# A decoder layer's attention projection in rounded products, its MLP weights in sixteen pieces, and identity products at the start

## The chip, the cores and the metric

The kernel runs on one core of one Trainium2 chip. The metric is the device time of one execution in microseconds; the time before is 995.11 us, the median of 3 runs (992.35 to 997.25).

## The reference, cut to what matters

Three blocks, each added to the stream x of shape (4, 512, 256). The first is a gated linear recurrence, the second an attention-free mixing block with an MLP, the third the two-layer local-attention block, which the change is about:

```python
def _layer(x, wqkv, qs, ksc, wo, lg, lb, w1, b1, w2, b2):   # twice, on layernorm(x)
    h = shift_token(x); q, k, v = split(h @ wqkv, 3)         # 8 heads of 64
    q, k = rotary_xpos(l2norm(q) * qs, l2norm(k) * ksc)
    o = local_attention(q, k, v)                             # windows of 128, one window back
    x = x + o @ wo                                           # wo: 512 x 256
    h = layernorm(shift_token(x)) * lg + lb
    a, g = split(h @ w1 + b1, 2)                             # 2 x 682 columns
    return x + (a * gelu(g)) @ w2 + b2
```

All arrays are fp32. In the kernel most products are made from operands split in two, a rounded part (hi, type fp32r) and the rest (lo): hi·hi + hi·lo + lo·hi, three rounded products in place of one full fp32 product.

## The kernel before, in words

All is written by hand: one instruction list for each engine, with semaphores; the order in each list is the order of execution. The activations stay in SBUF; 16 token tiles of 128 rows (4 sequences of 4 tiles) are the windows n of the attention. For each layer l the windows run first, n = 16 l to 16 l + 15, and then four MLP blocks m of 512 tokens. w = n mod 4 is the place in the sequence; at w = 0 a window has half the keys, so half the scores.

TensorE's `window` (L1943) holds, in order: the scores of n, the weighting of values of n-1, two of three qkv products of n+2, the transposes of keys of n+1, of probabilities, of queries of n+1, of the spread reciprocals of the row sums (`transpose_sums`), the third qkv product, the transpose of x for n+3, and last the projection `project_o` of n-1 (L1932 to L1941): four full fp32 products of 128 x 128 by 128 x 256. After the last window come `weigh_values` and `project_o` once more, the waits for the MLP's weights, and the MLP loop.

VectorE's `window` (L1071) masks the scores, writes o_t of n-1 (`normalise`, L1063), norms the keys of n+1 (L1039), inverts the row sums, makes the rotary products of n+2, and adds the projection to the residual (L1069). GpSimd's `window` (L601) copies an x tile (L543), spreads the inverted sums (L558), adds the rotary halves (L551), computes the inverse norms (L569, a power) and the queries' norm (L573), and at w = 1 to 3 splits a third of a quarter of the MLP's weights (L576 to L585): 12 pieces of 356 columns a layer. After the windows it zeroes a row, and `last_columns` (L592) copies the last 42 columns of w1. ScalarE makes the exponentials and most copies out of PSUM.

SyncE issues all DMAs from one list (L364 to L385): the four quarters of the MLP's weights, each into `w_stage` after the quarter before is split; the shifts of the residual by one token (`shift`, L342, lines L351 and L352); `stack_weights` (L319), which puts parts of w2's last rows into one tile; the next layer's qkv and output weights (`load_att`, L306); and after each MLP block's first step `stack_last` (L335), which TensorE waits for before L2017. At the start TensorE waits for the identity (L1664), transposes the first normalised batch, and multiplies it with W_in (`inputs`, L1605); GpSimd splits the gate weights (L437, L439) with the second batch's rstd (L411) between the first and second pair.

Of the kernel before, what the change touches and what calls it, by code (L numbers as in the profile page):

```python
# [41 lines left out]
WM_PIECES = 3  # L42
WM_PIECE = 356
# [32 lines left out]
def build(nc, x, ctx_in, cols_in, rows_in, w_in, w_gate, w_out, wq, wk, wv, wo_x, pos_bias,  # L76
          w1_x, w2_x, lcols_in, qk_scale, rope, wqkv, wo_l, wm_l, out):
    with ExitStack() as ctx:
# [3 lines left out]
        def signals(names):  # L82
# [21 lines left out]
        w_stage = sb("w_stage", [P, KD * 3 * INNER])  # L104
# [3 lines left out]
        wo_sb = sb("wo_sb", [P, KI, D])  # L108
# [100 lines left out]
        o_t = sb("o_t", [P, KI, P], stack=st_att)  # L209
# [3 lines left out]
        probs_t_far = w_stage[:, 2 * KD * INNER:4 * KD * INNER // 2 + 2 * 4 * P].rearrange(  # L213
            "p (i c t) -> p i c t", i=2, t=P)
        probs_ts = [(probs_t, probs_t_far)[i // 2][:, i % 2, :, :] for i in range(KI)]
        st_att.close()
# [32 lines left out]
        (rope_in, wqkv_in, wo_in, wm_in, wq_hi, wq_lo, wm_copied, wm_split, c_xt_lo, d_full, d_in_hi, d_in_lo,  # L249
         d_hi) = signals(  # L250
            "rope_in wqkv_in wo_in wm_in wq_hi wq_lo wm_copied wm_split c_xt_lo d_full d_in_hi d_in_lo d_hi")
# [25 lines left out]
        def _(sp):  # L277
# [28 lines left out]
            def load_att(l):  # L306
                if l:
                    sp.wait_ge(c_pv, l * NT)
                sp.dma_start(w_stage[:, :], wqkv[l].rearrange("p k n -> p (k n)")).then_inc(wqkv_in, 16)
                if l:  # L310
                    sp.wait_ge(c_wo, l * NT)
                sp.dma_start(wo_sb[:, :, :], wo_l[l]).then_inc(wo_in, 16)

            def load_mlp(l, b):

                sp.dma_start(w_stage[:, 0:WM_QUARTER], wm_l[l, :, b * WM_QUARTER:(b + 1) * WM_QUARTER])\
                    .then_inc(wm_in, 16)

            def stack_weights(l):  # L319

                hi, lo = (w[:, W1_COLS + (KH - 1) * D:W1_COLS + KH * D].bitcast(F32) for w in (wm_hi, wm_lo))
                dst = w2_last[:, :].bitcast(F32)
                sp.wait_ge(wm_split, WM_PIECES * NB * (l + 1))
# [64 lines left out]
        def _(pool):  # L388
# [187 lines left out]
            def split_mlp_weights(l, b, piece):  # L576

                m = l * NB + b
                src = w_stage[:, piece * WM_PIECE:(piece + 1) * WM_PIECE]
                dst = bass.ds(b * WM_QUARTER + piece * WM_PIECE, WM_PIECE)  # L580
                wait_alone(pool, wm_in, 16 * m + 16)
                pool.tensor_copy(wm_hi[:, dst], src).then_inc(wm_copied, 1)
                pool.wait_ge(wm_copied, WM_PIECES * m + piece + 1)
                pool.tensor_tensor(wm_lo[:, dst], src, wm_hi[:, dst].bitcast(F32), ALU.subtract)\
                    .then_inc(wm_split, 1)  # L585
# [6 lines left out]
            def last_columns(l):  # L592

                pool.wait_ge(wm_split, WM_PIECES * NB * (l + 1))
# [5 lines left out]

            def window(n, t, w, l, b, two, three):  # L601
                if three:
                    copy_tile(n + 3, t + 3, (w + 3) % 2, l * NB + b + 1 if w == 0 else l * NB + b + 2)
                spread_sums(n)
# [6 lines left out]
                if w:  # L611
                    split_mlp_weights(l, b, w - 1)
# [33 lines left out]
            for l in range(LAYERS):  # L646
# [941 lines left out]
        def _(pe):  # L1588
# [75 lines left out]
            pe.wait_ge(ready_consts, 1)  # L1664
            transpose_in(0)
# [266 lines left out]
            def project_o(n, keyed):  # L1932

                pe.wait_ge(c_ot_out, n + 1)
# [4 lines left out]
                for k in range(KI):  # L1939
                    ins = pe.matmul(bank[2][:, 0:D], o_t[:, k, :], wo_sb[:, k, :], start=(k == 0), stop=(k == KI - 1))  # L1940
                ins.then_inc(c_wo, 1)  # L1941

            def window(n, w, l, prev, one, two, three):  # L1943
# [22 lines left out]
                if prev:  # L1966
                    project_o(n - 1, one)
# [99 lines left out]
            for l in range(LAYERS):  # L2067
                n0 = l * NT
                ahead(l, 7)
                pe.wait_ge(wo_in, 16 * l + 16)  # L2070
# [11 lines left out]
                project_o(n0 + NT - 1, False)  # L2082
                pe.wait_ge(wm_split, WM_PIECES * NB * (l + 1))
# [87 lines left out]
```

## Time and profile before

| | |
|---|---|
| median of 3 runs | 995.11 us (992.35 to 997.25) |
| profiled execution: its time, its span | 999.37 us, 997.6 us |
| mean granted TensorE clock | 0.979 |
| VectorE, ScalarE, GpSimd busy | 674.6, 513.4, 419.3 us |
| attention of layer 0 and layer 1 | about 367 to 578 us and 689 to 895 us |

The page's slices, 40 equal parts of the span, each digit a busy share in tenths; PEclk is the granted clock of TensorE in tenths of full speed:

```
POOL 5333354113121367666666400007676767631110
PEclk9889998999999988999999999999999999989999
```

GpSimd is at 6 to 7 tenths in the attention of both layers and nearly idle in the MLPs. Times in rows are microseconds from the span's start; a duration of a TensorE row runs to the modelled end of the pipeline, so consecutive products overlap, and the distance of their starts is what one costs.

### The profile page before, as it was taken

The numbers are of one execution on the slowest core, as the hardware profiler recorded it, in microseconds if no ns is written. First come the engines' busy times: TensorE is split into PE (matmuls) and PEld (weight loads), VectorE is DVE, ScalarE is ACT, GpSimd is POOL, SyncE is SP. The second block draws the span as 40 slices with busy tenths as digits, with TensorE's granted clock in tenths as the row PEclk, the third lists the DMA queues.
The fourth block names the chain that finished last, engine by engine and source line by source line (L and its number), as shares of the span: only waits on it lengthen the run. The fifth ranks groups of instructions, "written<-read, shape, count | busy, mean of one in ns | idle before, by whom it ended". The sixth has DMA issues, their size and how long they took to land.

```text
span 997.6 us, 17519 instructions
## 1 busy us (share of the span) xinstructions
PE 927.7 (93%) x5688; PEld 776.2 (78%) x5688; DVE 674.6 (68%) x1706; ACT 513.4 (51%) x1221; POOL 419.3 (42%) x420
## 2 busy tenths in 40 slices
PE   5889996999999988999999799999999999889998
PEld 4668875787878867888888678887888888778887
DVE  6778697568687677666777555567776767735553
ACT  5466751313131416767676634454766666654443
POOL 5333354113121367666666400007676767631110
PEclk9889998999999999999999999999999999989999
DMA  7100123000000000000001030000000000000001
GB/s 267 62 1 27 37 64 111 0 2 0 0 1 1 2 21 1 2 22 0 22 0 33 13 103 14 4 26 1 2 24 0 22 0 20 20 14 16 31 24 46
DMA packets 15716, 26.34 MB, mean 26 GB/s; under 512 B 1642, under 2 KB 12256, under 8 KB 14896
## 3 DMA queue, kind: packets, MB, share of 16 engines
q1 hardware_dynamic: 15664, 25.69, 7.9%
q8 instruction: 27, 0.44, 0.2%
q14 instruction: 25, 0.20, 0.1%
HBM read 20.53 MB, written 2.10 MB: 23 GB/s over the span
## 4 chain that ended last, share of the span: by engine, by line
PE 70%; DVE 10%; ACT 8%; issue 4%; POOL 3%; SPq 3%; DMA 2%; ACTq 0%; DVEq 0%; POOLq 0%
PE bank L1592 32%; PE bank L1940 6%; PE bank L1894 5%; PE bank L1800 5%; PE bank L1918 5%; ACT probs L1460 3%; PE bank L1904 3%; PE bank L1881 2%; PE bank L1763 2%; PE bank L1746 1%; PE bank L1928 1%; SPq L352 1%; DVE y L820 1%; PE bank L2013 1%; PE bank L2010 1%
## 5 line engine op out<-in xcount | busy, mean ns | idle before, releaser
L1460 ACT ACTIVATE probs<-bank,row_min 128x256 f32<-128x256 f32 (+1 forms) x256 | 110.4, 458 | 122.2 <-DVE row_min L1048 122.2
L569 POOL TENSOR_TENSOR norms<-norms,minus_half 128x16 f32<-128x16 f32 x32 | 93.6, 2924 | 2.7
L1048 DVE CUSTOM_DVE_ANT_0 bank<-bank,mask 128x256 f32<-128x256 f32 (+1 forms) x256 | 90.7, 425 | 5.7 <-PE bank L1894 5.6
L1592 PE MATMUL bank<-wqkv_hi,x_hi 128*128 128x512 f32 x192 | 82.3, 429 | 1.8 <-DVE rot L1024 1.1
L1592 PE MATMUL bank<-wqkv_lo,x_hi 128*128 128x512 f32 x192 | 76.4, 398 | 0.0
L1592 PE MATMUL bank<-wqkv_hi,x_lo 128*128 128x512 f32 x192 | 75.6, 394 | 0.0
L1185 DVE SCALAR_TENSOR_TENSOR hidden<-bank,lcols,hidden 128x512 f32<-128x512 f32 (+1 forms) x48 | 36.0, 749 | 51.0 <-PE bank L1592 28.3
L1069 DVE TENSOR_TENSOR inner<-inner,bank 128x256 f32 (+1 forms) x32 | 13.5, 421 | 82.0 <-PE bank L1940 82.0
L1904 PE MATMUL bank<-ident,probs 128*128 128x128 f32 x448 | 62.0, 280 | 3.9 <-ACT probs L1460 3.9
L551 POOL TENSOR_TENSOR q_tok<-rot 128x512 f32<-128x512 f32 x32 | 41.2, 1287 | 57.6 <-DVE rot L1024 57.6
L1592 PE MATMUL bank<-t_lo,wm_hi 128*128 128x512 f32 x160 | 63.6, 397 | 0.0
L1592 PE MATMUL bank<-t_hi,wm_hi 128*128 128x512 f32 x160 | 63.6, 397 | 0.0
L1940 PE MATMUL bank<-wo_sb,o_t 128*128 128x256 f32 x256 | 61.5, 383 | 2.0 <-DVE o_t L1063 1.7
L1592 PE MATMUL bank<-t_hi,wm_lo 128*128 128x512 f32 x160 | 62.7, 392 | 0.0
L1894 PE MATMUL bank<-k_t,q_t 64*128 64x256 f32 (+1 forms) x512 | 57.9, 366 | 0.7 <-ACT q_t L1447 0.7
L1800 PE MATMUL bank<-w,ff 128*128 128x256 f32 x256 | 56.7, 379 | 0.0
L1904 PEld LDWEIGHTS bank<-ident,probs 128*128 128x128 f32 x448 | 52.5, 144 | 4.9 <-ACT probs L1460 4.9
L558 POOL COPY rsum_heads<-row_rsum 128x512 f32<-128x512 f32 x32 | 19.6, 614 | 86.4 <-DVE row_rsum L1055 58.5
L1460 ACT ACTIVATION_READ_ACCUMULATOR probs<-bank,row_min 128x1 f32 x256 | 55.5, 217 | 0.0
L1894 PEld LDWEIGHTS bank<-k_t,q_t 64*128 64x128 f32 x512 | 43.4, 189 | 13.9 <-issue 10.7
L1800 PEld LDWEIGHTS bank<-w,ff 128*128 128x128 f32 x256 | 48.5, 190 | 6.6
L1019 DVE TENSOR_TENSOR rot<-bank,rope_l 128x512 f32<-128x512 f32 x64 | 43.8, 685 | 13.7 <-ACT squares L1431 13.7
(253 smaller groups left out, 2663.6 us busy)
## 6 DMA issues: line engine op xcount, KB each, us to landing
w_stage<-in_wm_l_dram SPq DMA_DIRECT2D x8, 534.0 KB, 3.5
w_stage<-in_wqkv_dram SPq DMA_DIRECT2D x2, 1536.0 KB, 8.2
out_dram<-stream SPq DMA_DIRECT2D x8, 256.0 KB, 2.4
emb<-in_ctx_dram SPq DMA_DIRECT2D x1, 1536.0 KB, 6.7
inner<-in_w_gate_dram SPq DMA_DIRECT2D x1, 1152.0 KB, 10.0
stream<-in_x_dram SPq DMA_DIRECT2D x2, 512.0 KB, 5.6
stream<-in_x_dram SPq DMA_DIRECT2D x1, 1024.0 KB, 12.4
ew<-in_pos_bias_dram SPq DMA_DIRECT2D x1, 1024.0 KB, 11.3
```

Of the source, the lines that this page charges most:

```text
L551: pool.tensor_tensor(dst[:, par, :], rot[:, 2 * i, :], rot[:, 2 * i + 1, :], ALU.add)\
L569: pool.tensor_tensor(norms[:, 2, :], norms[:, 1, :], minus_half[:, :], ALU.pow).then_inc(c_rn, 1)
L1019: dve.tensor_tensor(rot[:, 2 * i, :].rearrange("p (h d) -> p h d", d=DH), src, cos, ALU.mult)\
L1048: dve.tensor_tensor_reduce(logits, logits, mask[:, 2 * P - nk:2 * P], 1.0, FAR, ALU.add, ALU.min, row_min[:, w % 2, 2 * i + e:2 * i + e + ...
L1185: dve.scalar_tensor_tensor(hidden[0:r, i % 2, :], up[0:r, :], lcols[0:r, l, L_B1A + j:L_B1A + j + 1], hidden[0:r, i % 2, :], ALU.add, ALU. ...
L1460: act.activation(probs[:, i, e, 0:nk], logits, ACT.Exp, bias=row_min[:, w % 2, h:h + 1], scale=-1.0, accum_out=row_sum[:, w % 2, h:h + 1]) ...
L1592: ins = pe.matmul(out, stationary, moving, start=(first and i == 0), stop=(last and i == len(terms) - 1))
L1800: ins = pe.matmul(bank[6 + t // 2][:, (t % 2) * D:(t % 2 + 1) * D], ff[:, k, t * P:(t + 1) * P], w_2[:, k, :], start=(k == 0), stop=(k == ...
L1894: ins = pe.matmul(bank[SCORES[i // 2] + e][:, (i % 2) * 2 * P:(i % 2) * 2 * P + nk], q_t[half, i, :], k_t[half, i, k0:(w + 1) * P], start= ...
L1904: ins = pe.transpose(bank[SCORES[i // 2] + i % 2][:, (2 * e + k) * P:(2 * e + k + 1) * P], probs[:, i, e, k * P:(k + 1) * P], ident[:, :])
L1918: ins = pe.matmul(bank[3][e * DH:(e + 1) * DH, i * P:(i + 1) * P], v_tok[:, w - nk + 1 + k, h * DH:(h + 1) * DH], probs_ts[i][:, 2 * e + k ...
L1940: ins = pe.matmul(bank[2][:, 0:D], o_t[:, k, :], wo_sb[:, k, :], start=(k == 0), stop=(k == KI - 1))
```

## The change

The projection reads o_hi, o_lo, wo_hi and wo_lo: twelve rounded products instead of four full ones. GpSimd makes the four tiles: `split_wo` in a layer's first window, `split_o` of window n-1 in window n before `spread_sums`, and once more after the last window. o_lo lies where o_t lies and wo_lo where wo_sb lies, so the subtractions are in place; wm_stage, wo_hi and half of the transposed probabilities lie where w_stage lies. The MLP's weights come in 16 loads of 267 columns a layer, each loaded after the piece before is split, one piece in every window; the first shift stands between loads 7 and 8, the second after load 15. The next layer's wqkv load waits for all projections instead of all weightings. TensorE makes 16 products of the identity with itself before the first transposes.

```diff
-WM_PIECES = 3
-WM_PIECE = 356
+WM_PIECES = 4
+WM_PIECE = 267
...
             def load_att(l):
                 if l:
-                    sp.wait_ge(c_pv, l * NT)
+                    sp.wait_ge(c_wo, l * NT)
                 sp.dma_start(w_stage[:, :], wqkv[l].rearrange("p k n -> p (k n)")).then_inc(wqkv_in, 16)
-                if l:
-                    sp.wait_ge(c_wo, l * NT)
                 sp.dma_start(wo_sb[:, :, :], wo_l[l]).then_inc(wo_in, 16)
...
+            def load_mlp(l, i):
+
+                if i:
+                    sp.wait_ge(wm_split, 2 * (WM_PIECES * NB * l + i))
+                sp.dma_start(wm_stage[:, 0:WM_PIECE], wm_l[l, :, i * WM_PIECE:(i + 1) * WM_PIECE]).then_inc(wm_in, 16)
...
-                for b in range(NB):
-                    if b:
-                        sp.wait_ge(wm_split, WM_PIECES * (l * NB + b))
-                    load_mlp(l, b)
-                shift(l, 0)
+                for i in range(WM_PIECES * NB):
+                    if i == 2 * WM_PIECES:
+                        shift(l, 0)
+                    load_mlp(l, i)
                 shift(l, 1)
...
+            def split_wo(l):
+
+                pool.wait_ge(wq_lo, 6 * (l + 1))
+                pool.wait_ge(wo_in, 16 * (l + 1))
+                pool.tensor_copy(wo_hi[:, :, :], wo_sb[:, :, :]).then_inc(o_split, 1)
+                pool.wait_ge(o_split, 2 * NT * l + 2 * l + 1)
+                pool.tensor_tensor(wo_lo[:, :, :], wo_sb[:, :, :], wo_hi[:, :, :].bitcast(F32), ALU.subtract).then_inc(o_split, 1)
+
+            def split_o(n, l):
+
+                wait_alone(pool, c_ot_out, n + 1)
+                pool.tensor_copy(o_hi[:, :, :], o_t[:, :, :]).then_inc(o_split, 1)
+                wait_alone(pool, o_split, 2 * n + 2 * l + 3)
+                pool.tensor_tensor(o_lo[:, :, :], o_t[:, :, :], o_hi[:, :, :].bitcast(F32), ALU.subtract).then_inc(o_split, 1)
...
             def window(n, t, w, l, b, two, three):
                 if three:
                     copy_tile(n + 3, t + 3, (w + 3) % 2, l * NB + b + 1 if w == 0 else l * NB + b + 2)
+                if isinstance(t, int) and t == 0:
+                    split_wo(l)
+                else:
+                    split_o(n - 1, l)
                 spread_sums(n)
...
-                if w:
-                    split_mlp_weights(l, b, w - 1)
+                split_mlp_weights(l, b, w)
...
+                split_o(n0 + NT - 1, l)
                 zero_first(l)
                 last_columns(l)
...
             pe.wait_ge(ready_consts, 1)
+            for _ in range(16):
+                pe.matmul(bank[7][:, 0:P], ident[:, :], ident[:, :], start=True, stop=True)
             transpose_in(0)
...
-            def project_o(n, keyed):
-
-                pe.wait_ge(c_ot_out, n + 1)
+            def project_o(n, l, keyed):
+
+                pe.wait_ge(o_split, 2 * n + 2 * l + 4)
...
                 for k in range(KI):
-                    ins = pe.matmul(bank[2][:, 0:D], o_t[:, k, :], wo_sb[:, k, :], start=(k == 0), stop=(k == KI - 1))
+                    pe.matmul(bank[2][:, 0:D], o_hi[:, k, :], wo_hi[:, k, :], start=(k == 0), stop=False)
+                    pe.matmul(bank[2][:, 0:D], o_hi[:, k, :], wo_lo[:, k, :], start=False, stop=False)
+                    ins = pe.matmul(bank[2][:, 0:D], o_lo[:, k, :], wo_hi[:, k, :], start=False, stop=(k == KI - 1))
...
-                pe.wait_ge(wo_in, 16 * l + 16)
```

## Rows read from the trace of the kernel before

**Rows 1.** The page: busy us of each engine, share of the span, instructions.

```profile
PE 927.7 (93%) x5688; PEld 776.2 (78%) x5688; DVE 674.6 (68%) x1706; ACT 513.4 (51%) x1221; POOL 419.3 (42%) x420
```

**Rows 2.** The page: the chain that ended last, shares by engine.

```profile
PE 70%; DVE 10%; ACT 8%; issue 4%; POOL 3%; SPq 3%; DMA 2%; ACTq 0%; DVEq 0%; POOLq 0%
```

**Rows 3.** The chain's pieces in time (start, us, what): two projections.

```profile
472.03 1.73 PE bank L1940 x8
...
483.83 1.73 PE bank L1940 x8
```

**Rows 4.** Timeline of TensorE, layer 0's MLP: start, us, instruction.

```profile
621.10 0.28 PE L2009 MATMUL bank<-wm_hi,hidden_hi 128*128 128x256 f32 x1
...
622.75 0.28 PE L2013 MATMUL bank<-wm_hi,hidden_lo 128*128 128x256 f32 x1
```

**Rows 5.** Groups of instructions on GpSimd: count | busy, mean ns | idle before.

```profile
L551 POOL TENSOR_TENSOR q_tok<-rot 128x512 f32<-128x512 f32 x32 | 41.2, 1287 | 57.6 <-DVE rot L1024 57.6
...
L584 POOL TENSOR_TENSOR wm_lo<-w_stage,wm_hi 128x356 f32 x18 | 17.2, 954 | 3.0 <-POOL wm_hi L582 3.0
L475 POOL TENSOR_TENSOR a_b<-a_tok,rows 128x1024 f32<-128x1024 f32 x4 | 9.6, 2392 | 1.8 <-DVE a_tok L843 1.8
L582 POOL CAST wm_hi<-w_stage 128x356 f32 x18 | 8.6, 480 | 0.0
```

**Rows 6.** Timeline of a long window of layer 0, all engines.

```profile
451.58 0.69 DVE L1063 TENSOR_TENSOR o_t<-bank,rsum_t 128x512 f32<-128x512 f32 x1
...
452.19 0.68 DVE L1039 TENSOR_TENSOR k_tok<-k_tok,norms 128x512 f32<-128x512 f32 x1
...
454.43 0.61 POOL L558 COPY rsum_heads<-row_rsum 128x512 f32<-128x512 f32 x1 [2.22 <-issue]
...
456.59 0.60 PE L1928 MATMUL bank<-ident,rsum_heads 128*128 128x128 f32 x4
```

**Rows 7.** Line L1039 alone: ns min/median/max, first and last start.

```profile
L1039 DVE TENSOR_TENSOR k_tok<-k_tok,norms x32: 677/679/1567, 359.6 to 870.8; 128x512 f32<-128x512 f32 x32
```

**Rows 8.** Timeline of a short window (w = 0) of layer 0.

```profile
426.79 0.86 POOL L543 COPY x_tile<-inner 128x256 f32 x1
...
430.31 0.60 PE L1928 MATMUL bank<-ident,rsum_heads 128*128 128x128 f32 x4
```

**Rows 9.** Timeline of the first windows of layer 0 and of layer 1.

```profile
378.32 0.40 POOL L543 COPY x_tile<-inner 128x256 f32<-128x256 f32 x1
...
380.13 1.06 PE L1928 MATMUL bank<-ident,rsum_heads 128*128 128x128 f32 x4
...
692.52 0.86 POOL L543 COPY x_tile<-inner 128x256 f32<-128x256 f32 x1
...
695.89 0.60 PE L1928 MATMUL bank<-ident,rsum_heads 128*128 128x128 f32 x4
```

**Rows 10.** Timeline: the last projection of layer 0.

```profile
576.01 1.99 PE L1940 MATMUL bank<-wo_sb,o_t 128*128 128x256 f32 x8 [0.84 <-DVE o_t L1063]
```

**Rows 11.** Timeline: shifts in SyncE's DMA queue (SPq), and TensorE behind.

```profile
579.28 14.16 SPq L352 DMA_DIRECT2D shifted<-inner  x1
...
893.10 12.06 SPq L352 DMA_DIRECT2D shifted<-inner  x1
...
597.70 0.39 PE L2017 MATMUL bank<-w_last,last_in 128*128 128x256 f32 x1 [0.75 <-DMA last_in<-last_in]
```

**Rows 12.** Timeline of the start.

```profile
12.85 1.00 POOL L437 TENSOR_SCALAR w_gate_hi<-inner 128x768 fp32r<-128x768 f32 x1 [5.48 <-DMA inner<-in_w_gate_dram]
...
12.87 0.63 PE L1592 MATMUL bank<-t_lo,w_in_hi 128*128 128x512 f32 x1
...
17.16 5.66 DVE L689 TENSOR_SCALAR normed<-stream,mean_var,rstd 128x256 f32<-128x256 f32 x4 [0.91 <-POOL rstd L411]
```

**Rows 13.** Stretches: length, busy of PE, PEld, DVE, ACT, POOL, clock, DMA share, GB/s.

```profile
868.00:872.00 4.00, 1.46 (x25) 1.25 (x20) 3.50 (x16) 3.13 (x14) 1.48 (x3) 1.00 0.08 25
872.00:877.00 5.00, 5.00 (x30) 4.95 (x29) 0.49 (x5) 4.27 (x11) 3.18 (x5) 0.66 0.09 23
```

More of the change, by code:

```diff
@@ L103, in build @@
         inner = sb("inner", [P, NT, D])
-        w_stage = sb("w_stage", [P, KD * 3 * INNER])
+        st_stage = ExitStack()
+        w_stage = sb("w_stage", [P, KD * 3 * INNER], stack=st_stage)
+        st_stage.close()
+        wm_stage = sb("wm_stage", [P, 1024])
+        wo_hi = sb("wo_hi", [P, KI, D], F32R)
+        probs_t_far = sb("probs_t_far", [P, 2, 4, P])
         st_scan = ExitStack()
@@ L107, in build @@
         st_scan.close()
-        wo_sb = sb("wo_sb", [P, KI, D])
+        st_wo = ExitStack()
+        wo_sb = sb("wo_sb", [P, KI, D], stack=st_wo)
+        st_wo.close()
+        wo_lo = sb("wo_lo", [P, KI, D], F32R)
         qk_scale_sb = sb("qk_scale_sb", [P, LAYERS, 2, DH])
@@ L208, in build @@
         rsum_t = sb("rsum_t", [P, INNER], stack=st_att)
-        o_t = sb("o_t", [P, KI, P], stack=st_att)
+        st_o = ExitStack()
+        o_t = sb("o_t", [P, KI, P], stack=st_o)
+        st_o.close()
+        o_lo = sb("o_lo", [P, KI, P], F32R, stack=st_att)
         k_t = sb("k_t", [P, KI, T], stack=st_att)
@@ L212, in build @@
         probs_t = sb("probs_t", [P, 2, 4, P], stack=st_att)
-        probs_t_far = w_stage[:, 2 * KD * INNER:4 * KD * INNER // 2 + 2 * 4 * P].rearrange(
-            "p (i c t) -> p i c t", i=2, t=P)
         probs_ts = [(probs_t, probs_t_far)[i // 2][:, i % 2, :, :] for i in range(KI)]
+        o_hi = sb("o_hi", [P, KI, P], F32R, stack=st_att)
         st_att.close()
@@ L248, in build @@
             "d_shift d_stats d_aggr d_eps d_rstd d_norm d_tp d_tp_out d_w1 d_gelu d_act d_w2 d_res0")
-        (rope_in, wqkv_in, wo_in, wm_in, wq_hi, wq_lo, wm_copied, wm_split, c_xt_lo, d_full, d_in_hi, d_in_lo,
+        (o_split, rope_in, wqkv_in, wo_in, wm_in, wq_hi, wq_lo, wm_split, c_xt_lo, d_full, d_in_hi, d_in_lo,
          d_hi) = signals(
-            "rope_in wqkv_in wo_in wm_in wq_hi wq_lo wm_copied wm_split c_xt_lo d_full d_in_hi d_in_lo d_hi")
+            "o_split rope_in wqkv_in wo_in wm_in wq_hi wq_lo wm_split c_xt_lo d_full d_in_hi d_in_lo d_hi")
         (out_sum, out_sem) = signals("out_sum out_sem")
@@ L322, in stack_weights @@
                 dst = w2_last[:, :].bitcast(F32)
-                sp.wait_ge(wm_split, WM_PIECES * NB * (l + 1))
+                sp.wait_ge(wm_split, 2 * WM_PIECES * NB * (l + 1))
                 for row, src in ((0, hi[0:HLAST + 1, :]), (HLAST + 1, lo[0:FIT, :]), (L_LAST, hi[0:HLAST, :]),
@@ L578, in split_mlp_weights @@
                 m = l * NB + b
-                src = w_stage[:, piece * WM_PIECE:(piece + 1) * WM_PIECE]
+                src = wm_stage[:, 0:WM_PIECE]
                 dst = bass.ds(b * WM_QUARTER + piece * WM_PIECE, WM_PIECE)
-                wait_alone(pool, wm_in, 16 * m + 16)
-                pool.tensor_copy(wm_hi[:, dst], src).then_inc(wm_copied, 1)
-                pool.wait_ge(wm_copied, WM_PIECES * m + piece + 1)
+                wait_alone(pool, wm_in, 16 * (WM_PIECES * m + piece + 1))
+                pool.tensor_copy(wm_hi[:, dst], src).then_inc(wm_split, 1)
+                wait_alone(pool, wm_split, 2 * (WM_PIECES * m + piece) + 1)
                 pool.tensor_tensor(wm_lo[:, dst], src, wm_hi[:, dst].bitcast(F32), ALU.subtract)\
@@ L592, in last_columns @@
             def last_columns(l):
-                pool.wait_ge(wm_split, WM_PIECES * NB * (l + 1))
+                pool.wait_ge(wm_split, 2 * WM_PIECES * NB * (l + 1))
                 for dst, src in ((w1_last_hi, wm_hi), (w1_last_lo, wm_lo)):
@@ L1966, in window @@
                 if prev:
-                    project_o(n - 1, one)
+                    project_o(n - 1, l, one)
             def transpose_mlp(m):
@@ L2081, in _ @@
                 weigh_values(n0 + NT - 1, TT - 1)
-                project_o(n0 + NT - 1, False)
-                pe.wait_ge(wm_split, WM_PIECES * NB * (l + 1))
+                project_o(n0 + NT - 1, l, False)
+                pe.wait_ge(wm_split, 2 * WM_PIECES * NB * (l + 1))
                 pe.wait_ge(w1_last, 4 * (l + 1))
```

3 lines of the change are left out of this document (removed).

## The prediction

> **What bounds the kernel now.** I read the page's busy table, the chain of waits, then the timeline of one attention window on every engine. TensorE is busy for 93% of the span [rows 1], and 70% of the chain that ended last is TensorE [rows 2]. In the windowed attention (16 windows a layer, 32 in all) the output projection is in that chain in nearly every window, 1.73 us each [rows 3]. So time taken from a projection comes off the span, and a wait that TensorE gets there goes on it. VectorE, ScalarE and GpSimd work a window ahead or behind, each with some spare time. The questions are how much shorter twelve rounded products are than four full ones, and whether GpSimd can split the operands within its spare time.
>
> **The projection on TensorE.** Four fp32 products of 256 columns are eight records and take 1.73 us from their start to the next work [rows 3]. The MLP's second product already uses rounded products of this very shape; fourteen of them start between 621.10 and 622.75, 0.118 us apart [rows 4]. Twelve take 1.42 us, so a window loses 0.31 us, and 32 windows 9.9 us. The projection of the last-but-one window of each layer is followed by a wait for ScalarE anyway, so I count 30 of 32 in the loops' pace and keep 9.4 us.
>
> The Trainium skill bears on this term (Floating Point Precision, TensorE Precision Notes): true fp32 is four passes through the array. By that, three rounded products are three quarters of the time, 1.30 us, and the saving 0.43 us a window. The rows above decide: in them a rounded product costs a little over a quarter, and the sum does not use the page.
>
> **GpSimd in a steady window.** Added: rounding o_t (512 columns) and subtracting it. A GpSimd copy of 512 columns takes 0.61 us [rows 6]; a subtraction 1.29 us, as the equal-sized addition [rows 5]; with the gaps between dependent instructions about 2.2 us. The weight pieces go from three of 356 columns in three windows to four of 267 in four: at 0.48 + 0.95 us for 356 [rows 5] a piece of 267 is about 0.36 + 0.71, so three windows of four get 0.3 us less and the fourth (the short one, w = 0) 1.2 us more.
>
> split_o(n-1) stands ahead of spread_sums(n). It waits for o_t, written from 451.58 for 0.7 us; GpSimd is idle then, and spread_sums starts at 454.43 [rows 6]. Behind o_t VectorE runs the key norm, two SBUF inputs, from 452.19. That instruction takes 0.68 us as a rule and up to 1.57 beside GpSimd's work [rows 7], so I let GpSimd's copy wait for it: 452.9 to 455.1. spread_sums ends near 455.7, and TensorE wants its result at 456.59 [rows 6]: 0.9 us spare. The projection itself comes two microseconds later still. A long window costs nothing; with this cover gone it would cost what GpSimd is late.
>
> In the short window (11.8 us from projection to projection [rows 3]) GpSimd still copies x_tile at 426.79, while spread_sums followed at once; TensorE transposes at 430.31 [rows 8]. There split_o starts near 427.5, ends 429.7, spread_sums ends 430.4: about 0.2 us late in six such windows, 1.2 us; bounds 0 and 5 us. The extra weight piece makes the next window's rotation later, which has three microseconds to spare. TensorE's wait for o_split replaces that for o_t; behind it stand the next scores, and the split is ready some 3 us before.
>
> **Layer starts.** split_wo adds a copy and a subtraction of 1024 columns ahead of the first spread_sums. A subtraction of that size takes 2.39 us [rows 5]; the copy, by the slope between 356 columns at 0.48 and 512 at 0.61, 1.08 us; with gaps 3.65, and 0.7 for spread_sums behind it. In layer 0 GpSimd is free at 378.7, so the sums are spread at 383.0, while TensorE wants them at 380.13: 2.9 us. In layer 1 it is free at 693.4 and done at 697.7, against 695.89: 1.8 us [rows 9]. TensorE has nothing else in its order: 4.7 us. Bounds: 2.5 (a copy at VectorE's pace, overlap of the pair) and 6 us. The wait for wo_in that TensorE drops cost nothing, since the weights had landed long before.
>
> **Layer ends.** After the last window o_t is followed by the projection with nothing to cover it [rows 10]. Now 0.61 + 0.2 + 1.29 us of GpSimd stand between: 2.1 us twice, 4.2 us; bounds 3.6 and 5. The casts of the last columns stand behind that split and end beside the projection, hidden.
>
> **The DMA queue.** SyncE's loads of pieces come every window and have a whole window to land; the first shift now sits between pieces 7 and 8 and blocks the queue for some 13 us, which delays piece 8 by 1 to 2 us against ten to spare: nothing. Two things are not covered. The second shift is now behind load 15, hence behind the fourteenth window's split, so the stacking of w2_last starts some 3 us later and may end just after TensorE wants it. And the next layer's wqkv load waits for the last projection instead of for the last weighting, 4 us later; the shift behind it, already 14.16 us against 12.06 in layer 1 where no load precedes it, ends later, and TensorE already waits 0.75 us for the last_in stack behind it [rows 11]. Shift and stack end 4.4 us later than before, of which the late projection accounts for 2.0: 2.4 us more, in layer 0 alone. Bounds 0 and 4.5 us.
>
> **Identity products.** Sixteen in fp32 run from about 2 us, while TensorE has nothing to do; at the slow level they end near the first transposes. They should warm the clock: an early input product takes 0.63 us [rows 12]. But the chain at the start goes through the gate weights' landing at 12.8, GpSimd's split of them, and its rstd behind the first pair, on which VectorE's normalisation at 17.16 waits [rows 12]. Earlier input products end in a longer wait: 0; bounds -2.5 and +1.
>
> **Clock.** After 2.5 us of wait inside 868 to 872 the granted clock was 0.66 over the next 5 us, so 1.7 us were lost against full speed [rows 13]. There are now four new waits of 2 to 3 us; in layer 0 the same windows kept the full level. I enter 1.0 us; bounds -2 and +7.
>
> **Sum.** -9.4 + 1.2 + 4.7 + 4.2 + 2.4 + 0 + 1.0 = +4.1 us. The profiled execution took 999.4 us (span 997.6), 4.3 above the median of the runs; it would become 1003.5. Against the median 995.11: 999.2 us, 0.4% slower, just inside what a measurement of this kernel can tell from no change, about 0.5% or 5 us.
>
> **Rivals.**
> 1. GpSimd sets the pace (slower). If split_o with its waits needs over the 3.1 us that it has in a long window, everything behind it is late each time: transposed sums, and then TensorE. The point is 0.9 us beyond my estimate; each further 0.5 us costs 26 windows x 0.5 = 13 us, so 1012 us. For it: the key norm's 1.57 us shows how the two engines disturb each other. Against: in the long windows it ran undisturbed, since GpSimd was idle there.
> 2. The edges cost less (faster). If split_wo is hidden by window 0 and the queue's delay is absorbed, only -9.4 + 4.2 = -5.2 is left: 989.9 us. For it: GpSimd's durations are rough. Against: the start's rows leave no gap in TensorE's order.
> 3. The clock. The new waits make TensorE cold each time: 4 x 1.7 = 6.8 instead of 1.0, so 1005 us. For it: the stretch of rows 13. Against: the same windows at layer 0's end have waits too, and the page's clock line, shown with the profile above, has its highest digit there.
> 4. The identity products reach the end of the chain: 2.5 us off, 996.7 us. Against: rows 12.
> By the Trainium skill (TensorE: Matmul & The Clock Gate, What's actually happening) the throttled state is the default and activity releases it; that rule stands behind rivals 3 and 4, and the trace agrees with it at the start.
>
> **Chances.** Forecast 0.45, rival 1 0.2, rival 2 0.15, rival 3 0.15, rival 4 0.05. The forecast's case lies near the border: 0.34 of it within, 0.11 beyond; with rival 4 and parts of rivals 2 and 3 that gives faster 0.13, same 0.46, slower 0.41. Range 990 to 1009: it takes in rival 2's value and most of rival 1's.
>
> **What would show it.** Right: twelve products in 1.4 us per projection; in long windows no wait of TensorE before the transposed sums; waits of about 3 and 2 us there in the two first windows, and of 2 to 3 us before the last projection of each layer; the stall before the last_in product in layer 0 near 3 us; inputs earlier at the start but the second batch's products as late as before. Wrong: the period of a long window staying at 13.2 us or growing, or the second batch's products starting earlier.

## The result, and the profile after

The changed kernel took 1002.85 us (median of 20 executions, 999.20 to 1006.12), the kernel before beside it 997.12 us (20 executions, 992.35 to 999.91). The ratio is 1.0054, 95% interval 1.0042 to 1.0066: slower, by a little more than what can be told from no change. I had forecast 0.4% slower. The profiled executions differ by 4.1 us in span: 1001.7 against 997.6.

The page after, in the order of [rows 1, 2]: busy time by engine, then the chain that ended last.

```profile
PE 926.3 (92%) x5848; PEld 785.1 (78%) x5848; DVE 672.2 (67%) x1706; ACT 513.7 (51%) x1221; POOL 492.6 (49%) x504
...
PE 66%; DVE 10%; ACT 7%; issue 6%; POOL 6%; SPq 3%; DMA 2%; ACTq 0%; DVEq 0%; POOLq 0%
```

GpSimd has 73 us more work, and its share of the chain has doubled. Where it entered is told by TensorE's waits for GpSimd and for the DMA queue in the third block (total us, times, longest):

```profile
PE bank L1969 <- POOL o_lo L622: 5.7, 2, 2.9
...
PE bank L1957 <- POOL rsum_heads L566: 3.8, 2, 2.3
...
PE bank L2048 <- DMA last_in<-last_in: 2.4, 1, 2.4
```

Those are the layer ends, the layer starts and the stall behind the DMA queue, five places in all. The other 30 windows have no such wait. In the chain of waits a projection of the changed kernel reads as follows (start, us, what; answers to [rows 3]):

```profile
407.25 0.12 PE bank L1969
407.37 0.12 PE bank L1970
...
408.42 0.12 PE bank L1970
408.65 1.93 PE bank L1923 x16
```

It takes 1.40 us from its start to the next scores, where it took 1.73. Against the trace of before, TensorE reached the scores of the third window 0.2 us earlier (395.94, now 395.75) and those of the fourteenth 3.6 us earlier (536.87, now 533.23): 0.31 us a window over eleven windows. The MLP's second block began 3.9 us later than before (628.86, now 632.78). So all that the windows of layer 0 gave, and as much again, was lost between the last windows and that block.

The timeline there, and at the two starts (answers to [rows 9 to 11]):

```profile
376.61 1.04 POOL L613 CAST wo_hi<-wo_sb 128x1024 fp32r<-128x1024 f32 x1
377.74 2.35 POOL L615 TENSOR_TENSOR wo_lo<-wo_sb,wo_hi 128x1024 fp32r<-128x1024 f32 x1
380.03 0.61 POOL L566 COPY rsum_heads<-row_rsum 128x512 f32<-128x512 f32 x1
...
573.50 0.61 POOL L620 CAST o_hi<-o_t 128x512 fp32r<-128x512 f32 x1 [5.28 <-DVE o_t L1090]
574.18 1.26 POOL L622 TENSOR_TENSOR o_lo<-o_t,o_hi 128x512 fp32r<-128x512 f32 x1
575.50 0.39 PE L1969 MATMUL bank<-wo_hi,o_hi 128*128 128x256 f32 x1 [2.86 <-POOL o_lo L622]
...
577.05 0.63 PE L1619 MATMUL bank<-t_hi,w_last_hi 128*106 128x512 f32 x1
577.47 0.63 PE L1619 MATMUL bank<-t_lo,w_last_hi 128*106 128x512 f32 x1
...
579.81 16.06 SPq L361 DMA_DIRECT2D shifted<-inner  x1
```

Read the two lines of L1619 closely. These MLP products stand 0.42 us apart; from 580.4 on the same line's products stand 0.23 us apart. That is TensorE at its lower level, right behind the wait of 2.86 us. The stretches say the same (length, busy of PE, PEld, DVE, ACT, POOL, then the granted clock, DMA share, GB/s), of the changed kernel:

```profile
550.00:605.00 55.00, 45.67 (x293) 40.16 (x294) 23.66 (x75) 25.16 (x60) 12.58 (x21) 0.88 0.18 59
870.00:930.00 60.00, 51.91 (x345) 45.16 (x342) 29.10 (x89) 31.16 (x69) 18.38 (x25) 0.91 0.08 21
```

and of the kernel before:

```profile
550.00:605.00 55.00, 47.38 (x349) 39.90 (x348) 30.21 (x100) 28.70 (x66) 10.98 (x19) 1.00 0.16 55
870.00:930.00 60.00, 54.81 (x338) 46.78 (x339) 30.65 (x88) 32.58 (x69) 12.10 (x17) 0.94 0.06 17
```

Before, the end of layer 0 ran at the full level throughout. Now 12% of the clock is missing there. Part of it is missing before the waits that were added at the layer's end: both kernels have a wait of 2.54 us for k_tok in the last window but one of each layer. In layer 0 it ends at 555.93 in the kernel before and at 551.97 in the changed one, and the level stayed up behind the first and fell behind the second:

```profile
555.93 0.63 PE L1873 MATMUL bank<-ident,k_tok 128*128 128x128 f32 x4 [2.54 <-DVE k_tok L1039]
550.00:560.00 10.00, 7.17 (x77) 6.25 (x76) 6.27 (x32) 6.86 (x23) 6.17 (x9) 1.00 0.08 22
...
550.00:560.00 10.00, 8.04 (x56) 7.62 (x56) 3.98 (x18) 6.78 (x21) 5.07 (x7) 0.83 0.12 31
```

The third line is the changed kernel's. A fall to the lower level and back takes 1.7 us of full clock, so 0.0017 of the mean. At the two layer ends (540 to 610 us and 860 to 930 us) the trace of before has two such falls and the changed kernel's has seven. Three of the seven come with an added wait (577.0, 600.8 and 897.8), four come behind waits that the kernel before has too.

**Splitting the time into work and clock.** Every execution comes with its span and its mean granted clock. Within each kernel the two lie on a line. Over 191 executions of the kernel before, the changed one and ten kernels of the study (all but the two whose work is of another size), with an offset for each kernel, the slope is 6.8 us for 0.01 of mean clock. So I give below, beside each ratio, the mean clock and the span moved along that line to clock 0.984, "at a like clock". The 72 executions of the kernel before are those that ran beside the experiments. Every ± is a 95% interval of the mean over a kernel's executions; the uncertainty of the slope (± 0.3 us for 0.01) is not in it.

| kernel | runs | mean span | mean clock | at a like clock |
|---|---|---|---|---|
| before | 72 | 995.1 | 0.9840 ± 0.0006 | 995.0 ± 0.1 |
| changed | 20 | 1000.8 | 0.9758 ± 0.0009 | 995.2 ± 0.4 |

This is the main finding. At a like clock the change costs nothing that can be seen (+0.1 ± 0.4 us). It does not hang on the line alone: at 0.979, a clock that both kernels reach, ten executions of the kernel before have a mean span of 998.1 us and three of the changed one 998.0. The slower time is the lower clock: 0.0082, which is 5.6 us. The experiments ask which of the added waits brings it, and whether the terms of my sum were right one by one.

### The profile page after: what moved, and what is told of

Same layout as the page of the kernel before. It is cut to its first block, busy times and chain, and to the rows that moved or that the text cites. A ratio compares the mean times of both kernels' runs of the same rounds, so it can differ in the third digit from the quotient of the medians.

```text
span 1001.7 us, 18106 instructions
## 1 busy us (share of the span) xinstructions
PE 926.3 (92%) x5848; PEld 785.1 (78%) x5848; DVE 672.2 (67%) x1706; ACT 513.7 (51%) x1221; POOL 492.6 (49%) x504
## 4 chain that ended last, share of the span: by engine, by line
PE 66%; DVE 10%; ACT 7%; issue 6%; POOL 6%; SPq 3%; DMA 2%; ACTq 0%; DVEq 0%; POOLq 0%
PE bank L1619 30%; PE bank L1923 5%; PE bank L1829 5%; PE bank L1947 5%; PE bank L1933 3%; ACT probs L1487 3%; PE bank L1792 2%; PE bank L1969 2%; PE bank L1910 2%; SPq L361 2%; PE bank L1957 2%; PE bank L1970 2%; PE bank L1971 2%; PE bank L1775 1%; DVE y L847 1%
## 5 line engine op out<-in xcount | busy, mean ns | idle before, releaser
L1619 PE MATMUL bank<-wqkv_hi,x_hi 128*128 128x512 f32 x192 | 81.9, 427 | 1.9 <-DVE rot L1051 1.1
L1619 PE MATMUL bank<-wqkv_lo,x_hi 128*128 128x512 f32 x192 | 76.4, 398 | 0.0
L1619 PE MATMUL bank<-wqkv_hi,x_lo 128*128 128x512 f32 x192 | 75.7, 394 | 0.0
L1933 PE MATMUL bank<-ident,probs 128*128 128x128 f32 x448 | 64.1, 287 | 3.9 <-ACT probs L1487 3.9
L1619 PE MATMUL bank<-t_hi,wm_hi 128*128 128x512 f32 x160 | 63.9, 399 | 0.0
L1619 PE MATMUL bank<-t_lo,wm_hi 128*128 128x512 f32 x160 | 63.7, 398 | 0.0
L1619 PE MATMUL bank<-t_hi,wm_lo 128*128 128x512 f32 x160 | 62.8, 392 | 0.0
L1046 DVE TENSOR_TENSOR rot<-bank,rope_l 128x512 f32<-128x512 f32 x64 | 43.8, 685 | 13.8 <-ACT squares L1458 13.8
L1587 ACT ACTIVATE hidden_hi<-hidden 128x512 fp32r<-128x512 f32 x40 | 25.3, 633 | 49.5 <-DVE hidden L1212 49.5
## 6 DMA issues: line engine op xcount, KB each, us to landing
ew<-in_pos_bias_dram SPq DMA_DIRECT2D x1, 1024.0 KB, 11.5
```

The costliest lines, as they stand in the source:

```text
L1046: dve.tensor_tensor(rot[:, 2 * i, :].rearrange("p (h d) -> p h d", d=DH), src, cos, ALU.mult)\
L1587: act.activation(hi[0:r, :], hidden[0:r, i % 2, :], ACT.Copy).then_inc(d_hi, 1)
L1619: ins = pe.matmul(out, stationary, moving, start=(first and i == 0), stop=(last and i == len(terms) - 1))
L1933: ins = pe.transpose(bank[SCORES[i // 2] + i % 2][:, (2 * e + k) * P:(2 * e + k + 1) * P], probs[:, i, e, k * P:(k + 1) * P], ident[:, :])
```

## Experiments

**The identity products.** Edit: the loop is left out.

```
-            for _ in range(16):
-                pe.matmul(bank[7][:, 0:P], ident[:, :], ident[:, :], start=True, stop=True)
```

> The changed kernel without its 16 identity products; all else stays. My account: they end at 8.2 us, the TensorE then waits for its first transposes anyway, the inputs phase ended at 28.84 us with them and 28.77 us without, so the time stays within 0.1% of the changed kernel (ratio to the kernel before 1.004 to 1.006). Rival (they keep the clock up in the first 25 us and so pay for part of the rest): first input products slower and the end later by 1 to 2.5 us, ratio about 1.007. Second rival (they delay the transposes): 0.5 us faster.

Measured: ratio 1.0069 (1.0043 to 1.0094), six runs; clock 0.9768 ± 0.0029; 996.0 ± 0.4 at a like clock. That is 0.8 ± 0.5 us more than the changed kernel, and the ratio is the one that the first rival named. The same pair was measured again at the end, on the mended kernel:

> The kernel with the four mends, without the 16 identity products. The first run without them gave 0.8 us more than the changed kernel at a like clock, less than its own uncertainty. My account (they change nothing): within 0.1% of the kernel with the four mends, ratio to the kernel before 0.989 to 0.991. Rival (they are worth 0.8 to 2.5 us): ratio 0.991 to 0.993.

Measured: ratio 0.9911 (0.9885 to 0.9938) against 0.9899 (0.9875 to 0.9924) with them; 984.6 against 985.0 at a like clock. Here the sign is the other way. Taken together, the two pairs show no gain from the identity products. The changed kernel's first input product comes at 11.61 us where it came at 12.28, and then TensorE waits 2.7 us for VectorE's normed tile; the second batch starts at 28.84, before at 28.77.

**The sixteen pieces alone.** Edit, on the kernel before: pieces of 267 columns, one split a window, with the protocol of loads of the changed kernel; o_t and its weights stay whole.

```
-WM_PIECES = 3
-WM_PIECE = 356
+WM_PIECES = 4
+WM_PIECE = 267
```

> The kernel before with one part of the change alone: the MLP weights come in sixteen pieces of 267 columns, one a window, with the order of loads and of the shift transfers of the changed kernel; the way out of attention is in whole precision as before. My account: the pieces are hidden, except that the short windows carry one more split (0.2 us in 6 windows at most), so 0 to +1.2 us, ratio 1.000 to 1.001; the loads leave the DMA queue order near the layer's end nearly as before, and no wait of 2.4 us stands before the last MLP products of block 0 of layer 0. Rival (the pieces, through the later shift, make the queue stack at the layer's end and cost its cold stretch): +3 to +5 us, ratio 1.003 to 1.005, with that wait in the trace.

Measured: ratio 1.0039 (1.0022 to 1.0056), clock 0.9846, 998.7 ± 0.4 at a like clock: 3.6 us more than before. My figure of 0 to 1.2 us was wrong. The rival had the size and the late shift right, but the wait is for w_last and not for last_in, and the clock did not fall. The timeline at the end of layer 0:

```profile
557.15 11.47 SPq L353 DMA_DIRECT2D squares<-inner  x1
568.66 0.61 SPq L327 DMA_DIRECT2D w_last<-wm_hi  x1
...
575.40 0.48 PE L1591 MATMUL bank<-t_hi,w_last_hi 128*106 128x512 f32 x1 [1.86 <-DMA w_last<-wm_lo]
```

The second shift starts at 556.36, behind the sixteenth piece in SyncE's order. It holds the queue until 568.6, and only then are the last chunk's weights stacked. TensorE wants them right behind the last projection and waits 1.86 us, in layer 1 2.1 us. The changed kernel has the same late stacking and shows no wait for it, because TensorE already stands for o_lo in that time. To test this, the shift alone is moved:

```
                     if i == 2 * WM_PIECES:
                         shift(l, 0)
+                    if i == WM_PIECES * NB - 1:
+                        shift(l, 1)
                     load_mlp(l, i)
-                shift(l, 1)
```

> The kernel before with the sixteen pieces alone, and the second shift put ahead of the sixteenth piece in SyncE's list. My account: the 3.6 us that the pieces cost (at a like clock) are two waits of about 2 us for the stacked weights w_last, late because the second shift queues behind the sixteenth piece; with the shift first these waits are gone and the kernel is back at the time before: ratio 0.999 to 1.001. Rival (the pieces cost their time by their added splits or loads): ratio 1.003 or more, waits for w_last gone all the same.

Measured: ratio 1.0004 (0.9986 to 1.0021), 995.0 ± 0.4 at a like clock, no wait for w_last:

```profile
552.29 11.57 SPq L353 DMA_DIRECT2D squares<-inner  x1
563.91 0.42 SPq L318 DMA_DIRECT2D w_stage<-in_wm_l_dram  x1
569.06 0.63 SPq L327 DMA_DIRECT2D w_last<-wm_hi  x1
```

The piece lands 0.2 us after GpSimd could take it, and the stacking waits for its split alone. The whole price of the pieces was this one order in a queue. That is shown.

**The attention weights later in the queue.** Edit:

```
                 stack_weights(l)
-                if l < LAYERS - 1:
-                    load_att(l + 1)
                 for b in range(2, NB):
                     shift(l, b)
                     stack_last(l * NB + b - 2)
+                    if b == 2 and l < LAYERS - 1:
+                        load_att(l + 1)
```

> The changed kernel with the load of the next layer's attention weights moved in SyncE's list behind the third shift and the first stack of last_in. My account: the third shift's transfer falls from 16 us back to about 12 us, the wait of 2.40 us for last_in at 600 us falls to 0.75 us or less, and the stretch at the lower clock that follows it (600 to 605 us, granted clock 0.66) goes: 2.4 to 4 us faster than the changed kernel, ratio to the kernel before about 1.002. Rival (TensorE catches up the 2.4 us later, or the clock falls somewhere else by the same amount): no change against the changed kernel, ratio 1.005. Second rival (the attention weights now come too late for the rounding in the last MLP block): a new wait at 650 us, slower.

Measured: ratio 1.0032 (1.0016 to 1.0048), clock 0.9762, 992.8 ± 0.5 at a like clock: 2.4 us less work than the changed kernel. The shift takes 12.21 us again where it took 16.06, and there is no wait for last_in above 0.3 us in the trace. So the transfer part of my account is as expected, while its second half fails: the clock did not come back (0.9762 against 0.9758). In the trace, which is of the slowest of the twelve executions, the fall at 600 us is gone, but there are others elsewhere, as the rival had it for the clock. The same edit on the kernel before:

> The kernel before with only the load of the next layer's attention weights moved behind the third shift and the first stack of last_in. It tells how much of the gain of the mended kernel a reordering of transfers gives without rounded projections. My account: the kernel before waits there 0.75 us, so 0 to 0.8 us faster, ratio 0.999 to 1.000. Rival (the attention weights beside the shift cost more than the wait shows): 2 us or more faster, ratio 0.998 or less.

Measured: ratio 0.9982 (0.9965 to 0.9998), 993.8 ± 0.2 at a like clock. It gives 1.2 us, some more than the visible wait of 0.75 us; where the rest comes from I did not find. So half of the 2.4 us is not the change's own: the kernel before pays it too.

**The output weights split early.** Edit: split_wo(l) leaves window 0 and stands ahead of the first rotation (layer 0) and behind the three tile copies (layer 1).

```
             copy_tile(1, 1, 1, 1)
+            split_wo(0)
             rotate(0, 0)
```

> The changed kernel with the split of the layer's output weights moved out of window 0 into idle time of GpSimd: ahead of the first rotation in layer 0, behind the three tile copies in layer 1. My account: the waits of 2.25 us and 1.53 us ahead of the first transposed sums of each layer go, 3.8 us faster than the changed kernel (ratio to the kernel before about 1.0015). Rival (the products behind those waits then wait for something else, such as the rotations or the query norm): less than 1.5 us of it comes back, ratio 1.004 or more.

Measured: ratio 1.0029 (1.0012 to 1.0046), clock 0.9779, 992.6 ± 0.2 at a like clock: 2.5 us less work. The two waits for rsum_heads (3.8 us) are gone. Of the 3.8 us, 1.3 are not gained; the result lies between my account and its rival. In the trace the wait for last_in grew from 2.40 to 2.85 us; I did not follow where the rest went. The pair of instructions now stands where GpSimd was idle:

```profile
344.43 1.04 POOL L613 CAST wo_hi<-wo_sb 128x1024 fp32r<-128x1024 f32 x1 [6.93 <-DVE wqkv_lo L1165]
345.56 2.37 POOL L615 TENSOR_TENSOR wo_lo<-wo_sb,wo_hi 128x1024 fp32r<-128x1024 f32 x1
347.88 1.29 POOL L559 TENSOR_TENSOR q_tok<-rot 128x512 f32<-128x512 f32 x1
```

**The last projection of a layer.** Edit: GpSimd's last split_o goes; ScalarE rounds, VectorE subtracts, and TensorE takes the eight products of o_hi first.

```
+                act.activation(o_hi[:, :, :], o_t[:, :, :], ACT.Copy).then_inc(o_split, 1)
...
+                dve.tensor_tensor(o_lo[:, :, :], o_t[:, :, :], o_hi[:, :, :].bitcast(F32), ALU.subtract).then_inc(o_split, 1)
```

> The changed kernel with the last projection of each layer fed another way: ScalarE rounds o_t, VectorE subtracts, and the TensorE takes its eight products of the rounded part while the subtraction runs. The run with the sixteen pieces alone showed that the transfers that stack the last chunk's weights now end late (they queue behind the second shift) and cost a wait of about 2 us a layer as soon as nothing else hides it. My account: the wait for o_lo (2.86 us, twice) falls to about 1.5 us, but the wait for w_last takes most of what it gives back: 0.5 to 1.5 us faster than the changed kernel at a like clock. Rival (the split alone holds the end): 2.5 to 3 us faster. On the clock: if the lower mean clock of the changed kernel (0.976 against 0.984) comes from this wait, it goes back up to 0.980 or more; if it comes from somewhere else it stays.

Measured: ratio 1.0019 (1.0003 to 1.0034), clock 0.9802 ± 0.0015, 994.0 ± 0.6 at a like clock. Its waits and the product behind the projection:

```profile
PE bank L2118 <- ACT o_hi L1612: 3.0, 2, 1.5
...
PE bank L1622 <- DMA w_last<-wm_lo: 2.7, 2, 2.1
...
575.84 0.47 PE L1622 MATMUL bank<-t_hi,w_last_hi 128*106 128x512 f32 x1 [2.14 <-DMA w_last<-wm_lo]
```

The wait for the split falls from 2.86 to 1.5 us and the one for w_last comes out from under it, as expected: 1.2 us of work. The clock rises by 0.0044 ± 0.0017, worth 3 us, more than half of what was missing. Then with the shift ahead of the sixteenth piece as well:

> The changed kernel with the last projection split on ScalarE and VectorE and the second shift ahead of the sixteenth piece; output weights and attention weights as in the changed kernel. My account: against the run with the split alone (ratio 1.0019) the waits for w_last (2.7 us in two places) go as well, so 2 to 2.7 us faster than that, ratio 0.999 to 1.000, mean clock 0.980 or more. Rival (the wait moves on to the stacked last_in 25 us later, since the third shift's transfer is as long as before): less than 1 us faster, ratio 1.001 to 1.002, and a wait for last_in above 3 us in the trace.

Measured: ratio 1.0016 (0.9997 to 1.0036), clock 0.9793, 992.9 ± 0.4 at a like clock. That is 1.1 us less than with the split alone, where I had expected 2 to 2.7. The rival is right: the waits for w_last are gone, and the one for last_in, 25 us later, is now 3.9 us long.

```profile
577.29 16.85 SPq L361 DMA_DIRECT2D shifted<-inner  x1
...
PE bank L2052 <- DMA last_in<-last_in: 3.9, 1, 3.9
```

TensorE arrives earlier, the queue does not.

**How much room GpSimd has.** Edit: work whose results nobody reads, 2.4 us by my estimate, behind the split of a piece in every window.

```
+                for i in range(2):
+                    pool.tensor_copy(wm_stage[:, 512 + 256 * i:768 + 256 * i], qk_scale_sb[:, :, :, :].rearrange("p a b c -> p (a b c)"))
+                pool.tensor_tensor(wm_stage[:, 320:328], mask[:, 0:8], minus_half[:, 0:8], ALU.pow)
```

> The changed kernel with 2.4 us of additional work on GpSimd in every window, behind its split of the MLP weights (two copies of 256 columns at about 0.40 us and a power of 8 columns at about 1.6 us; their results are not read). It tests how much room GpSimd has in a long window. My account (spare of 0.9 us in a long window): 1.5 us a window over some 22 long windows, 25 to 40 us slower than the changed kernel, with waits for rsum_heads in every window. Rival (TensorE alone sets the pace of the windows, GpSimd has 2.4 us to spare): under 3 us slower.

Measured: ratio 1.0475 (1.0451 to 1.0500), 42 us slower than the changed kernel, just beyond my range of 25 to 40. In the trace the added work holds GpSimd for 2.3 us in some windows and 2.8 in others, and TensorE waits:

```profile
PE bank L1961 <- POOL rsum_heads L566: 33.8, 24, 2.1
```

That is 30.0 us more in 22 more windows. The waits do not tell the room, the distance between windows does. From one window's transposed sums to the next one's, a long window takes 14.0 to 14.2 us in most cases where it took 12.9, and a short one 13.8 where it took 11.5. So of 2.8 us a long window absorbs about 1.5, and a short window absorbs nothing of 2.3. The lower mean clock (0.971) accounts for 3.5 of the other 12 us; the rest shows in the longer distances, and I did not divide it further.

**Fewer products.** Edit: project_o keeps only o_hi by wo_hi; the eight products with a small part are left out of the computation.

> The changed kernel with the projection of the way out cut to its four products of rounded by rounded, eight of twelve left out (so the small parts of o and of the weights don't count in the output); the splits on GpSimd stay. My account: TensorE sets the pace of the windows, each product costs its 0.118 us: 30 windows x 8 x 0.118 = 28 us and 2 us at the layer ends, 26 to 30 us faster than the changed kernel. Rival (GpSimd or the chain through the sums sets the pace): under 15 us. On the clock: if the rounded projection itself, with TensorE less busy, lowers the mean granted clock, it is lower still here (0.970 or less); if it comes from the waits that the change adds, it stays at 0.974 to 0.978.

Measured: ratio 0.9852 (0.9825 to 0.9879), clock 0.974; 21 us less work than the changed kernel where I expected 26 to 30. Its waits tell the difference: for rsum_heads 7.8 us in 8 places (3.8 in 2 in the changed kernel) and for w_last 4.2 us (none there). That is 8.2 of the 30 us. Six of those places are the short windows, with 0.7 us each: they take 11.5 us as in the changed kernel, while a long window falls from 12.9 to 12.0. The expected 0.118 us a product is right in the long windows; in the short ones GpSimd needs all of the 11.5 us, and nothing is gained. On the clock it decides little: 0.9742 ± 0.0022 is at the edge of what I expected if the clock comes from the waits, and the run has added waits of its own.

**All the mends together.** Edit: the last four (weights split early, attention weights late, last projection on ScalarE and VectorE, shift ahead of the sixteenth piece).

> The changed kernel with four mends: the output weights split early, the load of the next layer's attention weights behind the first stack of last_in, the last projection split on ScalarE and VectorE, and the second shift put ahead of the sixteenth piece of the MLP weights in SyncE's list, so that the stacked weights are not late. My account at a like clock: 2.6 (output weights) + 2.4 (attention weights) + 2.6 to 3 (last projections, now that the stacked weights are in time) = 7 to 8 us less work than the changed kernel, so below the kernel before by 6 to 8 us at its clock; and with the added waits gone the mean clock goes back to 0.982 to 0.985, ratio 0.992 to 0.994. Rival (the lower clock comes from the rounded projections and stays at 0.976): ratio 0.998 to 0.999. Second rival (the second shift, earlier, delays the sixteenth piece and with it the last window): no gain from the last projections, ratio 0.997 at the clock of before.

Measured: 986.78 us against 996.46, ratio 0.9899 (0.9875 to 0.9924); clock 0.9837, as before the change; 985.0 ± 0.3 at a like clock. It beats both kernels: 10 us under the kernel before, 15 under the changed one. The ratio is below the 0.992 to 0.994 that I expected: one by one the mends gave 2.4, 2.5 and 2.3 us of work, together 10.2. One mend had left a wait that another takes away, as that of 3.9 us for last_in above; I did not account for all of the 3 us. The five waits listed at the top have shrunk to two of 1.5 us:

```profile
PE bank L2119 <- ACT o_hi L1613: 3.0, 2, 1.5
```

and the stretches at the layer ends are nearly back at full clock:

```profile
550.00:605.00 55.00, 50.48 (x343) 43.69 (x344) 28.46 (x82) 29.82 (x60) 10.02 (x19) 0.97 0.18 59
870.00:930.00 60.00, 54.83 (x344) 47.08 (x343) 32.88 (x84) 30.78 (x58) 11.73 (x16) 1.00 0.10 27
```

Against the kernel before, its parts add up: -9.4 for the projections, -1.2 for the weights' place in the queue, +1.3 for two waits of 1.5 where 0.85 stood; -9.3, measured -10.0.

## Why the prediction was right, and where it was not

The direction and nearly the size were right: 0.54% against a forecast of 0.41%. The sum was right in part by opposite errors, so it is worth going through.

- **The projections, -9.4.** Right: 0.31 us a window in the trace, and the mended kernel gets all of it. That TensorE sets the pace of the long windows is what the cut to four products shows.
- **Short windows, +1.2.** Not there: no short window has a wait before the transposed sums. In the one at 420 to 433 us the copy of x_tile took 0.39 us, not 0.86 as in [rows 8]. But there is no room left either: any added work on GpSimd shows in these windows in full.
- **Long windows, 0 with 0.9 us to spare.** Right that they cost nothing; the room is larger than I said, about 1.5 us by the added load. This is what stood between the forecast and the first rival, and at 2.3 to 2.8 us of more work that rival came true.
- **Layer starts, +4.7.** The mechanism is right, with waits of 2.25 and 1.53 us against 2.9 and 1.8. Their worth is 2.5 us, by the run that takes them away; why it is less than the 3.8 us of waits is open.
- **Layer ends, +4.2.** The waits grew by 2.0 us each, as forecast. What I gave no price is the stacking of w2_last. I wrote that it "may end just after TensorE wants it" and dropped it. With the pieces alone it ends 2 us after, in both layers; in the changed kernel it cost nothing only because the other wait covers it. By itself it is the 3.6 us of the sixteen pieces.
- **The DMA queue, +2.4.** The mechanism is right, the size too large: I forecast 2.4 us on top of the 0.75 that was there, and the wait grew by 1.65, to 2.40. Moving the load gives 2.4 us in the changed kernel and 1.2 in the kernel before, so by these runs the change added 1.2.
- **Identity products, 0.** Right, as far as the runs can tell.
- **The clock, +1.0.** This is the term that was mis-sized. It is 5.6 us, within my bounds of -2 to +7, and close to the third rival's 6.8. The rival's mechanism is right in the main: the clock comes back with the waits (0.0044 ± 0.0017 with the last projections', 0.0021 ± 0.0019 with the layer starts', all of it in the mended kernel, which still has its rounded products). It is not right one for one: taking the stall for last_in away left the clock where it was. I argued that the windows at layer 0's end had waits before and stayed at the full level. They had one of 2.54 us, for k_tok, and they did stay, but that was one execution. Over the fourteen traces (one of each kernel) a fall came with this wait in 13 of 28 places. With the wait of 2.86 us for o_lo it came in 12 of 12 places, between 0.1 and 1.6 us behind its end. With 0.84 or 1.5 us before the same projection it came in none of 16. So the waits added at the layer ends were of the kind that lowered the clock each time, and the three falls that came with added waits in the changed kernel's trace are 0.0051 of the 0.0082.

The other terms add up to +3.1 and measured +0.1 ± 0.4 at a like clock. Too large were the short windows by 1.2, the starts by 2.2, the queue by about 1 and the ends by 0.2. That is 4.6, so some 1.6 us of cost in the changed kernel stand in none of my terms, and I did not find them. The clock took 4.6 more than I gave it. Had the clock stayed, the time would have been that of the kernel before, by the line above.

What stays open: 0.0031 of the lower clock, about two falls an execution. In the changed kernel's trace they would be among the four behind waits that the kernel before has too (two of 2.54 us for k_tok, two of 1.23 for probs in the window after). Whether the change makes a fall there more frequent is not shown: the k_tok wait had one in 2 of 8 places in the kernels with the whole projection and in 11 of 20 in the others, too few traces to tell from chance.

## What to carry to other kernels

In a kernel bound by one engine, price a new wait at a boundary twice: the wait itself, and what the clock loses behind it. One execution in which a like wait left the clock alone is no evidence that it always will. Compare executions at a like clock before judging an edit by its median; here the edit's work was neutral and its clock was not. And where a wait covers another, mending the one shows the other: list everything that the same instruction needs, with its time of arrival, before moving any of it.

## What the runs showed of the hardware

- A mean granted clock 0.01 lower costs 6.8 us of some 995. The same kernel varies by 0.003 (standard deviation) from execution to execution, which is 2 us and nearly all the scatter of its times: at a like clock the kernel before scatters by 0.5 us.
- By the Trainium skill (TensorE: Matmul & The Clock Gate, What's actually happening) the throttled clock is the state without activity. The traces agree in kind. The level fell with 12 of 12 waits of 2.86 us before a layer's last projection and with 5 of 5 waits of 2.4 to 3.9 us for last_in. It fell with 13 of 28 waits of 2.54 us for k_tok, and with none of 16 waits of 0.84 or 1.5 us before the last projection. In the run with the sixteen pieces alone it stayed up behind waits of 1.86 and 2.09 us for w_last.
- A shift's transfer over 127 partitions (254 KB) holds SyncE's queue for 11.5 to 13.1 us over all traces, and for 14 to 17 us when the 1.5 MB of attention weights go just ahead of it. The Trainium skill (DMA: Bandwidth & Descriptors, Why a DMA increments its semaphore by 16 and not by 1) says that such a transfer goes to a single DMA engine, since the number of engines must divide the 127 partitions. The trace agrees: the 16 engines' mean busy share is 0.07 from 559 to 569 us, where this transfer is alone, and one of sixteen would be 0.06. No run here changed the number of partitions.
- Twelve rounded products of 256 columns take 1.40 us and four whole ones 1.73: rounding saves a fifth of the products' time, and costs GpSimd 1.9 us for each operand of 512 columns (0.61 and 1.26) where nothing disturbs it, and 2.2 us at the median of the changed kernel's 32 windows (0.94 and 1.28).
